# A graph layer on one core: the dense products taken in two float32r parts instead of three bfloat16 parts, the count matrix built in two halves, and 98 instead of 88 node blocks done by matrix

## The reference

```python
# x: 12500 x 128 float32; src, dst, edge_type: 400000 edges, sorted by dst
Xs = X[src]
m_data = Xs @ W_data.T + b_data
m_ctrl = Xs @ W_control.T + b_control
msg = where(edge_types == 0, m_data, m_ctrl)
agg = segment_sum(msg, dst, num_segments=12500)
out = relu(agg + (X @ W_self.T + b_self))
return layernorm(x + out)            # over the 128 features
```

## Time and profile before

| | |
|---|---|
| median of 3 runs (lowest, highest) | 2782.12 us (2778.26, 2785.72) |
| the profiled execution's own time | 2784.88 us |
| its span in the profile | 2783.0 us |
| its mean granted PE clock | 0.96 of full speed |
| PE busy | 2364.6 us (85%) |
| POOL busy | 1691.7 us (61%) |
| DVE busy | 1266.1 us (45%) |
| ACT busy | 1224.5 us (44%) |

### The profile page before, as it was taken

One profiled execution on the slowest core, in us unless ns is written; L12 is line 12 of the kernel. 1 busy time (PEld: TensorE's weight loads), 2 busy tenths in 40 slices (PEclk: granted clock), 3 DMA queues, 4 the chain that ended last, 5 costly groups with the idle time before them and its releaser, 6 DMA issues.

```text
span 2783.0 us, 47819 instructions
## 1 busy us (share of the span) xinstructions
PE 2364.6 (85%) x17776; PEld 1301.3 (47%) x17776; DVE 1266.1 (45%) x4037; ACT 1224.5 (44%) x1997; POOL 1691.7 (61%) x1785
## 2 busy tenths in 40 slices
PE   3688888888888888888889888988888888888988
PEld 2344444544444444444445454444444444444444
DVE  8444444445444444444444454444444444444443
ACT  6344444444444444444444444444444444444443
POOL 6466665666666665666666666566666666656662
PEclk9899999999999999999999999999999999999999
DMA  7712222222222222222222222222222222222221
GB/s 191 223 47 67 71 72 59 73 68 74 72 73 71 73 72 62 74 69 75 71 72 73 69 75 71 63 69 73 74 69 73 71 73 72 69 61 72 71 75 34
DMA packets 150380, 211.42 MB, mean 76 GB/s; under 512 B 35298, under 2 KB 120725, under 8 KB 150147
## 3 DMA queue, kind: packets, MB, share of 16 engines
q0 software_dynamic: 83232, 170.57, 22.0%
q1 hardware_dynamic: 54177, 28.15, 3.7%
q10 hardware_dynamic: 12738, 9.60, 1.1%
HBM read 189.78 MB, written 18.41 MB: 75 GB/s over the span
## 4 chain that ended last, share of the span: by engine, by line
PE 44%; another core or an unknown queue 23%; ACT 14%; DVE 9%; issue 7%; DVEq 2%; DMA 1%; SPq 0%; ACTq 0%
PE apply_ps L664 25%; ACT cnt L860 13%; PE build L648 8%; PE sum_ps L630 4%; DVEq L1177 2%; DVE hot_q L1136 2%; DVE hot_p L1136 1%; PE misc L673 1%; DVE acc L1183 1%; PE misc L714 1%; DVE sg L1193 1%; PE misc L717 1%; DMA key_dram<-fin 1%; PE misc L692 1%
## 5 line engine op out<-in xcount | busy, mean ns | idle before, releaser
L560 POOL DMA_INDIRECT rows<-x_dram,src_t x1610 | 1524.7, 947 | 947.5 <-issue 383.4
L860 ACT ACTIVATE cnt<-build 128x784 bf16<-128x784 f32 x1408 | 1087.5, 822 | 1457.1 <-remote 773.1
L664 PE MATMUL apply_ps<-x,cnt 128*128 128x385 bf16 x8624 | 1611.2, 337 | 31.0 <-issue 25.5
L664 PEld LDWEIGHTS apply_ps<-x,cnt 128*128 128x128 bf16 x8624 | 868.3, 103 | 604.7 <-issue 135.7
L648 PE MATMUL build<-hot_q,hot_p 64*128 64x196 bf16 x5632 | 425.1, 254 | 274.2 <-ACT cnt L860 205.6
L648 PEld LDWEIGHTS build<-hot_q,hot_p 64*128 64x128 bf16 x5632 | 197.6, 95 | 572.7 <-issue 372.7
L1136 DVE TENSOR_TENSOR hot_q<-const_ps,key_pq 128x784 bf16<-128x784 bf16 x704 | 390.3, 554 | 0.0
L1181 DVE TENSOR_TENSOR acc_deg<-misc,acc_deg 2x32 f32 x346 | 61.9, 179 | 671.2 <-remote 278.7
L1136 DVE TENSOR_TENSOR hot_p<-const_ps,key_pq 128x512 bf16<-128x512 bf16 x704 | 291.2, 414 | 43.1 <-DVE acc L1183 16.5
L560 POOL DMA_INDIRECT rows<-in_x,src_t x120 | 122.8, 1024 | 76.8 <-issue 30.5
L1191 DVE TENSOR_TENSOR zg<-t_mask,sum_ps 128x2 f16<-128x2 f32 x161 | 24.9, 154 | 307.5 <-PE sum_ps L630 158.3
(11 more groups left out here) (182 smaller groups left out, 1082.5 us busy)
## 6 DMA issues: line engine op xcount, KB each, us to landing
rows<-x_dram,src_t POOLq DMA_INDIRECT x1610
x_dram<-x ACTq DMA_DIRECT2D x13, 672.0 KB
cnt<-in_x SPq DMA_DIRECT2D x13, 448.0 KB
x_u<-in_x SPq DMA_DIRECT2D x43, 64.0 KB
out<-out_sb SPq DMA_DIRECT2D x43, 64.0 KB
key_dram<-fin SPq DMA_DIRECT2D x12, 196.5 KB
x_u<-in_x SPq DMA_DIRECT2D x40, 53.5 KB
out<-out_sb SPq DMA_DIRECT2D x40, 53.5 KB
```

What stands on the lines that cost most here:

```text
L560: pool.indirect_dma_start(out=rows_f[:, slot, 0:D] if early else rows[:, slot, 0:ROW], out_offset=None, in_=x if early else x3_dram, in_of ...
L664: last = pe.matmul(apply_ps[:, 0:385], cnt[:, k % 2, b, :], x3[:, b, 0:385], start=(b == 0), stop=(b == XBLOCKS - 1))
L860: act.activation(o, i.rearrange("p h (m b) -> p b h m", b=XBLOCKS), ACT.Copy).then_inc(evacuated, 1)
```

## The change

x is held in SBUF in two float32r parts (`x2`, 256 columns and two columns of ones), high part by an ACT copy, low part by one DVE subtraction (`split_lo`). There is no middle part and no copy in DRAM; all gathers read float32 rows of x, and all rounds use the float32 matmul of 129 columns and `take_sums` on ACT. `cnt` is float32r and holds half of the source blocks (49) of one block of nodes in each buffer. A step's build handles 16 nodes for one half: 16 matmuls of 98 columns; `hot_p` is made once for both halves. A half takes 4 steps, a block still 8. The apply of a half is given out in portions of 6, 12, 12, 12 and 7 source blocks, the last of them at the head of the following step; it starts at step 4. 98 blocks (784 building steps) are done by matrix, and 157 rounds remain, one in about 5 steps, with two of a round's gathers behind each step. x is loaded through 7 buffers, the keys are made in 15 chunks. `hot` has two slots instead of three and is always float32; the outputs are normalised in place in `y_sb`.

```diff
-BLOCKS = 88
+BLOCKS = 98
-GATHER_0 = 1395
+GATHER_0 = 1555
-ROW = 3 * D
+ROW = 2 * D
-APPLY_AT = BUILD_AT + 8
+APPLY_AT = BUILD_AT + 4
+PORTIONS = (6, 12, 12, 12, 7)
-DKCH = 11
-QUARTER = (0, 0, 0, 1, 1, 2, 2, 2, 3, 3)
+DKCH = 15
+FIFTH = (0, 0, 1, 1, 2, 2, 3, 3, 4, 4)
...
-    gather_step = [4 * j for j in range(places) if j not in left_out][:PAIRS]
+    gather_step = [(BATCHES + APPLY_AT) * r // PAIRS for r in range(PAIRS)]
...
-        x3 = sb("x3", [P, XBLOCKS, 386], BF16)
-        cnt = sb("cnt", [P, 2, XBLOCKS, P], BF16)
+        x2 = sb("x2", [P, XBLOCKS, ROW + 2], F32R)
+        cnt = sb("cnt", [P, 2, HALF, P], F32R)
-        rows = sb("rows", [P, SLOTS, ROW + 2], BF16)
-        hot = sb("hot", [P, 3, 2 * GT, 2 * WIN])
+        rows = sb("rows", [P, SLOTS, D + 1])
+        hot = sb("hot", [P, 2, 2 * GT, 2 * WIN])
...
-                if ps == F32_ROUNDS:
-                    pool.wait_ge(x3_stored, 16 * (XCH + 1))
                 for i in range(2 * GT):
-                    if ps >= AHEAD and i and QUARTER[i] != QUARTER[i - 1]:
-                        n = gather_step[ps - AHEAD] + QUARTER[i]
+                    if ps >= AHEAD and i and FIFTH[i] != FIFTH[i - 1]:
+                        n = gather_step[ps - AHEAD] + FIFTH[i]
...
-                        out=rows_f[:, slot, 0:D] if early else rows[:, slot, 0:ROW],
-                        out_offset=None, in_=x if early else x3_dram,
+                        out=rows[:, slot, 0:D], out_offset=None, in_=x,
...
+                    last = pe.matmul(sum_ps[part, 0:D + 1], hot[:, ps % 2, st, :], rows[:, slot, 0:D + 1],
+                                     start=(j == 0), stop=(j == GT - 1))
...
+                    for j in range(4 * z, 4 * z + 4):
+                        pair, r = divmod(j, 2)
                         for h in range(2):
+                            part = slice(64 * h, 64 * h + 64)
+                            o = WIDE * h + 2 * HALF * (j % 4)
+                            last = pe.matmul(build_ps[z][:, o:o + 2 * HALF], hot_p[part, 4 * q4 + pair, :, r],
+                                             hot_q[part, 4 * (n % 3) + pair, :, r], start=True, stop=True)
...
+            def apply(y, c):
+                k, half = divmod(y, 2)
                 if c == 0:
-                    pe.wait_ge(evacuated, 16 * (k + 1))
-                    if k:
+                    pe.wait_ge(evacuated, 8 * (y + 1))
+                    if half == 0 and k:
                         pe.wait_ge(posted, k)
...
+                b0, b1 = sum(PORTIONS[:c]), sum(PORTIONS[:c + 1])
+                for i in range(b0, b1):
+                    b = half * HALF + i
+                    last = pe.matmul(apply_ps[:, 0:ROW + 2], cnt[:, half, i, :], x2[:, b, :],
                                      start=(b == 0), stop=(b == XBLOCKS - 1))
...
             for s in range(STEPS):
+                y, c = divmod(s - APPLY_AT, 4)
+                if c == 0 and 0 < y <= 2 * BLOCKS:
+                    apply(y - 1, 4)
                 if s in gather_at:
                     gather_sums(gather_at[s])
...
-                if gather_at.get(s, PAIRS) < F32_ROUNDS:
+                if s in gather_at:
                     take_sums(gather_at[s])
                 if batch_at(s) is not None:
                     evacuate(batch_at(s))
...
             def evacuate(n):
+                y, q4 = divmod(n, 4)
+                if q4 == 0 and y >= 2:
+                    act.wait_ge(applied, y - 1)
+                if n == 4:
+                    act.wait_ge(x2_ready, XCH)
                 for z in range(2):
                     act.wait_ge(built, 2 * n + z + 1)
+                    c0 = 32 * q4 + 16 * z
+                    o = cnt[:, y % 2, :, c0:c0 + 16].rearrange("p b (h m) -> p b h m", h=2)
+                    i = build_ps[z][:, :].rearrange("p (h c) -> p h c", h=2)[:, :, 0:8 * HALF]
+                    act.activation(o, i.rearrange("p h (m b) -> p b h m", b=HALF), ACT.Copy
                                    ).then_inc(evacuated, 1)
...
             def make_onehots(n):
+                k, half, q4 = n // 8, n // 4 % 2, n % 4
+                if half == 0:
+                    dve.tensor_tensor(
+                        hot_p[:, 4 * q4:4 * q4 + 4, :, :], table_p.unsqueeze(1).to_broadcast([P, 4, P, 2]),
+                        keys_p.unsqueeze(2).to_broadcast([P, 4, P, 2]), ALU.is_equal)
...
-                if F32_ROUNDS <= gather_at.get(s, 0):
-                    add_parts(gather_at[s])
```

More of the change, by code:

```diff
@@ L9 @@
 F32 = mybir.dt.float32
+F32R = mybir.dt.float32r
 BF16 = mybir.dt.bfloat16
@@ L20 @@
 WIN = 32
-TYPE_STEP = 16384
 EPS = 1e-5
@@ L64, in gnn_resnorm @@
     assert (TILES - GATHER_0) % (2 * GT) == 0 and BLOCKS % 2 == 0 and XBLOCKS % XB == 0 and DENSE > WIN_0
[L65 to L69, removed]
-    gather_step = [4 * j for j in range(places) if j not in left_out][:PAIRS]
-    assert len(gather_step) == PAIRS
+    assert KEY_TILES % DKCH == 0 and SLOTS == AHEAD * 2 * GT and sum(PORTIONS) == HALF
+    gather_step = [(BATCHES + APPLY_AT) * r // PAIRS for r in range(PAIRS)]
     taken = set()
@@ L169, in sb, with under @@
             return ctx.enter_context(nc.sbuf_tensor(name, shape, dt))
+        def under(name, shape):
+            with nc.sbuf_tensor(name, shape, F32) as t:
+                return t
         def sem(name):
@@ new lines, in gnn_resnorm @@
+        xs_all = cnt_raw[:, 1, :, :].rearrange("p b c -> p (b c)")
+        xs = [xs_all[:, XB * D * i:XB * D * i + XB * D] for i in range(XS)]
+        x2f = x2[:, :, :].bitcast(F32)
+        off_i = acc_deg[32:33, :, :].rearrange("p e w -> p (e w)").bitcast(I32)[:, 0:GROUPS]
+        iotas = hot_p[:, :, :, :].rearrange("p s q r -> p (s q r)").bitcast(I32)
+        iota_q, iota_p = iotas[:, 0:2 * XBLOCKS], iotas[:, 2 * XBLOCKS:2 * XBLOCKS + P]
+        iota_i, hot_i = iotas[:, 512:768], iotas[:, 768:768 + 2 * WIN]
@@ L457, in _ @@
                     load_window(1)
-                    for i in range(3):
-                        load_unit(i, units[i].n0, units[i].r)
             for c in range(1, DKCH):
@@ L463, in _ @@
                     load_dkeys(c + 2)
+            sp.wait_ge(dkeys_written, 16 * (DKCH + 1))
+            for i in range(3):
+                load_unit(i, units[i].n0, units[i].r)
             for s in range(STEPS):
@@ L625, in gather_sums @@
                     part, st = slice(64 * g, 64 * g + 64), g * GT + j
-                    if ps < F32_ROUNDS:
-                        last = pe.matmul(sum_ps[part, 0:D + 1], hot[:, ps % 3, st, :], rows_f[:, slot, 0:D + 1],
-                                         start=(j == 0), stop=(j == GT - 1))
-                    else:
-                        last = pe.matmul(sum_ps[part, 0:ROW + 1], hot_b[:, ps % 3, st, :], rows[:, slot, 0:ROW + 1],
-                                         start=(j == 0), stop=(j == GT - 1))
+                    last = pe.matmul(sum_ps[part, 0:D + 1], hot[:, ps % 2, st, :], rows[:, slot, 0:D + 1],
+                                     start=(j == 0), stop=(j == GT - 1))
@@ L661, in apply @@
                 if k == 0:
-                    pe.wait_ge(x3_ready, -(-b1 // XB))
-                for b in range(b0, b1):
-                    last = pe.matmul(apply_ps[:, 0:385], cnt[:, k % 2, b, :], x3[:, b, 0:385],
+                    pe.wait_ge(x2_ready, -(-(half * HALF + b1) // XB))
+                for i in range(b0, b1):
+                    b = half * HALF + i
+                    last = pe.matmul(apply_ps[:, 0:ROW + 2], cnt[:, half, i, :], x2[:, b, :],
                                      start=(b == 0), stop=(b == XBLOCKS - 1))
-                if c == 7:
+                if c == 4:
```

298 lines of the change are left out of this document (107 added, 191 removed).

## The result

The changed kernel takes 2672.70 us, the median of three runs (2671.38 to 2673.01), against 2782.12: a ratio of 0.9606, 95% interval 0.9584 to 0.9628. It is 3.9% faster (these runs of the two kernels are called the first pair). I had said 2460 us and 11.6%.

The account below looks back on a forecast made before the run. PE's own work bounds 85%, a hand-over to ACT most of the rest. A step of 2.63 + 0.41 = 3.04 us gives 126 + 760 x 3.04 + 21 = 2457, predicted 2460 us; range 2290 to 2700.

Parts of the forecast that it names:

- The sum for the kernel before: PE's own work in an average step before: apply, build, rounds, block turn and units, 3.09 us at full clock.
- the build: PE's 16 build matmuls of 98 columns in a step: 0.46 to 0.59 us, taken as 0.52.
- the round: PE's matmuls of a gather round, all float32 now: 1.26 us in place of 0.94.
- the start: Time up to step 24: it begins at 126 us instead of 153, with the first apply at 55 us.
- the end: Time after the last build: 21 us instead of 36.8.
- Rival 2: Apply matmuls slower, through an unhidden wide weight load or two cycles a column: 3410 or 3530 us; chance 0.10.
- Rival 3: ACT's wide stores slow: a build's copy takes 1.72 us, a step about 3.8, the time 3035 us; chance 0.05.
- Rival 4: PE's waits vanish: residue 0.10 us, step 2.73 us, time 2225 to 2300 us; chance 0.10.
- I take 0.120: Each apply matmul of 258 columns: 0.1075 us of stream plus 0.012 overhead, longer weight load hidden; apply 1.49 us a step.
- So I scale it: 0.59 x 0.69 = 0.41: Residue per step after: shrinks with a group of 12 apply matmuls, from 2.07 to 1.43 us.
- the residue: Part of a step beyond PE's summed work, waiting and what the sum misses: 0.59 us before, 0.41 forecast.
- Rival 1: Hand-over of builds to ACT doesn't shrink: residue 0.59 to 0.72 us a step, 2594 to 2693 us; chance 0.25.

Follow-up runs that it names:

- quiet series: Later series of runs in which the kernel before took 2313 to 2315 us; the changed kernel, unaltered, took 2268.31 us there, ratio 0.9805.
- The runs with late signals: Each kernel with a build's signal moved to the second and third last matmul of the apply group behind it: before 3639.60 us, changed 3462.59.

## Why the prediction missed

1. **What held.** The sum for the kernel before (3.09 us a step at full clock) was right: 3.11 at a clock of 1.00. So were the build (0.49 for 0.52), the round (1.26), the copy of 822 ns, the start within 13 us and the end within 2. Rivals 2, 3 and 4 fall: 0.1215 us a matmul, 822 ns a copy, and a step of 3.30 us instead of 2.73.
2. **The first step that failed is "I take 0.120", in the apply's term (1.49 against 2.11).** The pace of 0.120 is nearly right inside a group, at 0.1215. But the 0.012 of overhead that I carried over from the timeline of 385 columns was an average that spread a group's exit over its matmuls (in the quiet trace of the kernel before they start 0.166 us apart, and the last one of a group has 0.258). By that trace 0.006 would have been the overhead inside a group, where the new format has 0.014, so that 0.120 came out near is luck. And the longer load was said to hide always, which it doesn't behind a build, whose matmuls each use one half of the rows (row-tiled). With 0.18 for each group a step's apply is 12.25 x 0.1215 + 0.18 = 1.67 us, 0.18 more than forecast; 0.07 came back: 0.03 in the build, the rest in turns (0.21 us from 1508.44 to 1508.65, for 0.28) and units. In the quiet series that makes 2.67 x 0.99 = 2.64 us against 2.53 at full clock. The rule of the Trainium skill (TensorE: Matmul & The Clock Gate, "What overlaps and what doesn't"), by which each apply matmul would take an estimated 0.21 us, does not agree with these rows: inside a group loads of 193 ns on average go with a matmul every 0.1215 us, so full-array loads overlap there.
3. **Of the first pair's 0.23 us of own work**, 0.12 is this (0.11 over the clock of 0.95) and 0.03 the granted clock of 0.95 for 0.96. The rest, 0.08, comes with the first pair's series, and the kernel before had as much: 0.10 us of its 0.59 were busy time beyond the sum (3.32 for 3.22). The rows account for it in the main: the changed kernel's builds hold 515.7 us there and 452.4 in the quiet series, 0.08 us a step, since builds broken by a wait last longer. The apply's rows grow as well (1436.5 for 1367.1), with stretches at the lower clock as at 1498.06.
4. **The second step that failed is "So I scale it: 0.59 x 0.69 = 0.41".** The 0.59 were 0.49 us of idle time and 0.10 of busy time. The same two are 0.44 and 0.08 after, 0.52 together (the 0.67 less the apply's 0.12 and the clock's 0.03) and not 0.41. So the residue fell to 0.88 of what it was, and the difference of 0.11 us a step, 84 us, weighs nearly as much as the apply's 0.12. With the clock's 0.03 they make up the 0.26. The runs with late signals show why the length of the group is the wrong rule: once a copy starts at the group's end, PE waits for the copies. That the idle time alone came out near 0.41 is luck. Rival 1, with 0.25, had this mechanism, but its 0.59 to 0.72 for the residue was too much; its range (2594 to 2693) holds the time only because the apply's miss came on top, and the stated range holds it because that rival was taken in.
5. **What I had not asked** is what the ten blocks do by themselves. A block costs PE 8 steps (2.36 us each without rounds in the new format) and saves 1.6 rounds. Ten of them are 8.1% of the time in the old format, and 0.3% in the new one, where POOL is the limit with 88. Of the versions that were run, the one with six more blocks is the fastest.
6. **Why 3.9% there and 2.0% in quiet series.** The first pair's conditions add 0.49 - 0.02 us of idle time to each of 680 steps before, 324 us, and 0.44 - 0.12 to each of 760 after, about 238 us, since the changed kernel already waited some in the quiet series. PE's busy time rises by nearly the same in both, 141.1 and 154.0 us.

What stays open is the source of the unnamed waits, 773 us in the first profile of the kernel before and none in the quiet series, at the same busy times of ACT and POOL. Late signals were made by hand; what makes them late in the first pair was not found.

## What to carry to other kernels

Fit a timeline's groups of different length with a cost for each matmul and one for each group before you carry an overhead to a format with shorter streams: the second part does not shrink. Where a copy waits for the end of a group, cost PE's wait by the copy, not by the group. Measure a residue after the change in the terms in which it was taken before. A change that moves work between two engines and makes one of them cheaper is two changes; run both alone, and from both ends, since here the format was worth 9.3% with 98 blocks and 1.6% with 88.

## What the runs showed of the hardware

A float32r matmul of 258 columns with 4-byte weights goes at 0.1215 us and one with bfloat16 halves at about 0.117 (from 0.80 and 1.50 us for 6 and 12), though the loads last 193 and 100 ns. Behind row-tiled matmuls the entry of a group with 4-byte weights costs about 0.09 us more than with 2-byte ones; behind a float32 transpose the group begins as much earlier (0.09 us behind the transpose in place of 0.17). At the lower clock level the same matmuls start 0.214 us apart. One and the same kernel took 2315, 2782 and 2814 us in different series, and one chip number appears with 2314 and with 2814; in the profiles of 2783 and 2314 us ACT, DVE and POOL are busy within 0.6% of each other, PE is busy 2364.6 and 2223.5 us, and the granted clock is 0.96 and 0.99.
